# A fused attention and mixture-of-experts layer on one core: three edits to the order of work in its first pass

## The reference

```python
x = x + _layernorm(attn(_layernorm(x)))     # RWKV-like attention
x = x + _layernorm(moe(_layernorm(x)))      # 8 experts, the best 2 of each token, and one shared MLP

# attention: xk, xv, xr are mixtures of x and x shifted by one token
k, v, r = xk @ Wk.T, xv @ Wv.T, xr @ Wr.T
sr = sigmoid(r)
# scan over the tokens, a and b carried per channel
eku = exp(u + kt); out = (a + eku * vt) / (b + eku)
ek = exp(kt);      a, b = a * ew + ek * vt, b * ew + ek
attn = (sr * out) @ Wo.T

# moe: top 2 of softmax(x @ gate_w.T + gate_b); each expert and the shared MLP:
h = silu(x @ w1.T + b1) * (x @ w3.T + b3);  y = h @ w2.T + b2
```

## Time and profile before

| | us |
|---|---|
| median of 3 runs | 1219.38 |
| lowest, highest | 1210.02, 1220.20 |
| the profiled execution | 1216.82 |
| its span, first to last instruction | 1215.0 |
| TensorE busy (matmul) | 1007.6 (83%) |
| DVE busy | 847.6 (70%) |
| POOL busy | 795.2 (65%) |
| ACT busy | 569.0 (47%) |
| mean granted clock of TensorE | 0.922 |

### The profile page before, as it was taken

The page is one execution under the profiler, slowest core; times in us unless marked ns, Lnnn a source line. Parts: engine busy times, 40 slices in busy tenths (PEclk is TensorE's granted clock), DMA queues, the critical chain, the costliest instruction groups (busy, mean ns, idle before and its releaser), DMA issues. The chain is left out here.

```text
span 1215.0 us, 23017 instructions
## 1 busy us (share of the span) xinstructions
PE 1007.6 (83%) x6344; PEld 890.1 (73%) x6344; DVE 847.6 (70%) x2227; ACT 569.0 (47%) x1013; POOL 795.2 (65%) x790
## 2 busy tenths in 40 slices
PE   0567799999999999999997784979998999989562
PEld 0456678777877788778876674979998999988432
DVE  4577797778787888778876323746775766766496
ACT  4333664456555654565455423424443434433275
POOL 2233877787778777887787432447775766655498
PEclk9778999999999999999998877989998999999655
DMA  3223332453235423442243118588878888887496
GB/s 132 72 96 97 104 108 83 138 160 125 73 123 160 130 81 118 152 143 91 96 135 105 62 68 286 135 218 200 155 136 220 161 197 193 188 209 192 104 262 223
DMA packets 114548, 174.05 MB, mean 143 GB/s; under 512 B 13485, under 2 KB 93768, under 8 KB 112200
## 3 DMA queue, kind: packets, MB, share of 16 engines
q1 hardware_dynamic: 83304, 121.09, 32.9%
q0 software_dynamic: 26592, 35.67, 15.8%
q10 hardware_dynamic: 4608, 16.78, 3.7%
HBM read 173.53 MB, written 78.21 MB: 207 GB/s over the span
## 5 line engine op out<-in xcount | busy, mean ns | idle before, releaser
L1497 POOL DMA_INDIRECT sum_y<-e_y,e_row_at x142 | 222.5, 1567 | 44.2 <-issue 40.7
L1331 PE MATMUL e_h_ps<-e_z_hi,e_w 128*128 128x256 f32 x1136 | 222.6, 290 | 29.1 <-DMA e_w<-w_split 17.5
L1331 PEld LDWEIGHTS e_h_ps<-e_z_hi,e_w 128*128 128x128 f32 x1136 | 187.1, 197 | 31.9 <-issue 22.4
L1331 PE MATMUL e_h_ps<-e_z_lo,e_w 128*128 128x256 f32 x568 | 163.7, 288 | 0.0
L1373 ACT ACTIVATE e_act_h<-e_h_ps,e_w 128x256 f32<-128x256 f32 x142 | 67.3, 474 | 205.6 <-PE e_h_ps L1331 182.8
L1152 POOL DMA_INDIRECT slots_x<-f_xf,f_at x128 | 140.3, 1096 | 32.4 <-issue 32.4
L615 PE MATMUL f_h_ps<-f_f_hi,f_w_hi 128*128 128x512 f32 x256 | 108.9, 425 | 27.7 <-DVE f_h L909 23.8
L1412 DVE SCALAR_TENSOR_TENSOR e_h<-e_h_ps,e_w,e_act_h 128x256 f32<-128x256 f32 x142 | 68.1, 483 | 75.7 <-ACT e_act_h L1373 63.1
L1347 PE MATMUL e_y_ps<-e_w,e_h_hi 128*128 128x256 f32 x568 | 118.4, 292 | 1.1 <-DVE e_h_lo L1419 1.1
L876 DVE RECIPROCAL f_den<-f_den 128x256 f32<-128x256 f32 x64 | 111.6, 1746 | 1.1
L1331 PEld LDWEIGHTS e_h_ps<-e_z_lo,e_w 128*128 128x128 f32 x568 | 111.9, 197 | 0.0
(11 more groups left out here) (222 smaller groups left out, 2971.3 us busy)
## 6 DMA issues: line engine op xcount, KB each, us to landing
e_w<-w_split SPq DMA_DIRECT2D x71, 1026.0 KB
e_w<-w_split ACTq DMA_DIRECT2D x71, 512.0 KB
e_x_in<-slots_x SPq DMA_DIRECT2D x71, 260.0 KB
f_x_in<-x SPq DMA_DIRECT2D x16, 512.0 KB, 5.0
f_x_res<-x SPq DMA_DIRECT2D x16, 512.0 KB, 5.9
x_dram<-f_x SPq DMA_DIRECT2D x16, 512.0 KB, 6.6
sum_y<-f_y SPq DMA_DIRECT2D x32, 256.0 KB, 3.0
c_x<-x_dram SPq DMA_DIRECT2D x32, 256.0 KB
```

The lines of the kernel that those rows point to most:

```text
L1331: last = pe.matmul(h_ps[q][:, which, :], w13(p, part)[:, which, c, q * P:(q + 1) * P], z[p % 2][:, c, :], start=(n == 0), stop=(n == 5))
L1497: pool.indirect_dma_start(out=dst[:, :], out_offset=bass.IndirectOffsetOnAxis(ap=row_at[p][:, j:j + 1], axis=0), in_=y[p][:, j, :], in_off ...
```

## The change

Five places in `first_pass`:

- DVE: `product(i - 2, 2)` moves ahead of `denominator(i, 1)`; the second half's reciprocal becomes one instruction of 512 columns behind `low(i + 1)`, instead of one half in front of the product and one behind `low`. The count that `gate` waits for goes with it, from 4 to 3 per sequence.
- DVE and ACT: `low_w` and `high_w` move from the end of the step to its start, `low_w` behind `moments_x`, `high_w` behind the first `f_high`.
- SP: the stores of the split weights move ahead of the loads of `x_in` and `x_res`, the store of x1 and the `zs` transfers; the load of `w_raw` moves to the end of the body and is for the next step.
- Pool: `running_sums(i, 1)` and `inverse_std` of the third norm move ahead of the hold and the first two scatters.

```diff
@@ SP
             def body(i, par):
-                if inside(i, SEQS):
-                    wait(sp, w_stored, 64 * i)
-                    sp.dma_start(w_raw[:, :], expert_w[:, bass.ds(i * HALF_W, HALF_W)]).then_inc(w_loaded, 16)
...
+                if inside(i, SEQS):
+                    half = i % 2 if isinstance(i, int) else par
+                    sp.wait_ge(w_lo_ready, i + 1)
...
+                n = i + 1
+                if inside(n, SEQS):
+                    wait(sp, w_stored, 64 * n)
+                    sp.dma_start(w_raw[:, :], expert_w[:, bass.ds(n * HALF_W, HALF_W)]).then_inc(w_loaded, 16)
@@ ACT
                 f_high(i - 2, par, 0)
+                high_w(i)
                 exps(i, 0)
...
                 read_y(i - 3, 1)
-                high_w(i)
                 h_high(i - 2, 0)
@@ DVE
-                dve.wait_ge(rec_ready, 4 * s + n)
+                dve.wait_ge(rec_ready, 3 * s + n)
...
                 moments_x(i + 1, 1 - par)
+                low_w(i)
                 f_low(i - 2, par, 1)
...
                 aggregate(LN_X1, i - 1, 1 - par)
+                product(i - 2, 2)
                 denominator(i, 1)
-                invert(i, 1, slice(0, T // 2))
-                product(i - 2, 2)
-                low_w(i)
                 low(i + 1)
-                invert(i, 1, slice(T // 2, T))
-                gate(i, 1, 4)
+                invert(i, 1, slice(0, T))
+                gate(i, 1, 3)
@@ POOL
                 add_x(i - 1, 1 - par)
+                running_sums(i, 1)
+                inverse_std(LN_X1, i - 1, 1 - par)
                 if inside(i - 2, SEQS):
                     hold(pool, scratch, held, i - 2, (at_ready, i - 1))
                 send(i - 2, par, 0, (0, 1))
-                running_sums(i, 1)
-                inverse_std(LN_X1, i - 1, 1 - par)
```

More of the change, by code:

```diff
@@ L466, in body @@
                             .then_inc(y_stored[half], 16)
+                if inside(i, SEQS):
+                    half = i % 2 if isinstance(i, int) else par
+                    sp.wait_ge(w_lo_ready, i + 1)
+                    for low, words in ((0, w_high[:, :].bitcast(F32)), (1, w_raw[:, :])):
+                        if half == 0:
+                            at = i * (W_ALL // 2) + low * W13
+                            sp.dma_start(w_split[:, bass.ds(at, HALF_W)], words).then_inc(w_stored, 32)
+                        else:
+                            at = (i - 1) * (W_ALL // 2)
+                            sp.dma_start(w_split[:, bass.ds(at + low * W13 + HALF_W, W13 - HALF_W)],
+                                         words[:, 0:W13 - HALF_W]).then_inc(w_stored, 16)
+                            sp.dma_start(w_split[:, bass.ds(at + 2 * W13 + 4 + low * W2, W2)], words[:, W13 - HALF_W:])\
+                                .then_inc(w_stored, 16)
                 n = i + 2
```

## The result

| | before | after |
|---|---|---|
| median of all runs, us | 1216.58 | 1225.27 |
| lowest, highest | 1210.02, 1222.80 | 1222.71, 1233.62 |
| ratio, 95% interval | 1 | 1.0079 [1.0064, 1.0095] |
| span of the profiled execution | 1215.0 | 1225.3 |
| mean granted clock of TensorE | 0.922 | 0.909 |

The third of the projections starts at 140.83 after and at 147.10 before: filling the pipe gained 6.3 us, where 6.6 were forecast. The last one starts at 676.36 against 662.86: the middle has lost all that and 13.5 us more.

What follows compares the result with a forecast made beforehand. TensorE was taken to wait on DVE's order, then on Pool: a middle step falls from 39.70 to 38.65 us. Gains 2.5 + 3.1 + 1.0 + 12 x 1.05 = 19.2 us off 1216.8 give 1197.6, set at 1200; range 1186 to 1214.

Steps and rivals of the forecast that it cites:

- The two waits of TensorE: TensorE's waits in ten steps, 14.9 us for DVE's `f_h` and 7.2 us for `f_z_lo`; both were to go.
- that for `f_den`: DVE's denominator sat idle 2.26 us for Pool's `f_den`; that wait was to be gone.
- Filling the pipe: First steps of the first pass: gains of 2.5, 3.1 and 1.0 us in steps 0, 1 and 2.
- Pool idles 2.3 us for the scan: Pool, after its `f_x` addition, was to wait 2.3 us for `f_a_sum`, which follows DVE's scan.
- Pool's chain from the running sums to the end of `g_low`: Pool's work before the projection: 18.4 us was to shrink to 16.35 through fewer meetings with DVE.
- P+22.3: Middle step, counted from the projection's start P: when `f_a_sum` ends and Pool's running sums can start.
- P+38.7: Middle step, counted from the projection's start P: when Pool's chain lets the next projection start.
- the term for SP in the sum: SP's weight stores (issues of 1.1 to 1.8 us) fit its idle time ahead of `zs_hi`; counted as 0.
- Rival (b): First pass: thinner cover, late weights or `g_low` waiting for DVE; 8 us of gain left, 1211; chance 0.27.
- 1.5 us of waiting to spend: TensorE's expected wait for Pool in front of the projection, about 1.5 us, which delays could use up without cost.
- the clock was forecast to stand: TensorE's clock, at 1.00 with a wait of 1.54 us each step, should stay with a like wait elsewhere.
- The rival's late weights: Part of the 0.27 rival: weights landing late delay ACT's exponentials, the second `f_low` and the logits.

Runs made afterwards that it cites:

- e1: The changed kernel with the stores of the split weights first in SP's body, ahead of the stores of y; 1201.8 us, ratio 0.9887.
- e2: The changed kernel with the whole weight split (loads, stores, `high_w`, `low_w`) as before, `low_w` right ahead of `low`; 1203.5 us, ratio 0.9892.
- e12: The changed kernel with the `zs` transfers on ACT's queue and SP waiting for `f_z_lo` before the next weight load; 1233.2 us, ratio 1.0123.
- e8: The kernel before with Pool's part alone: running sums and scales ahead of the hold and first two scatters; 1213.2 us, ratio 0.9992.
- e7: The kernel before with DVE's part alone: product q=2 ahead of the denominator, whole reciprocal behind `f_z_lo`; 1196.3 us, ratio 0.9843.
- e3: The changed kernel with Pool's order as before: hold and two scatters ahead of the running sums; 1222.2 us, ratio 1.0027.
- e5: The changed kernel with the weight stores first on SP and Pool's order as before; 1189.2 us, ratio 0.9787.
- e6: The changed kernel with the stores of the split weights issued from ACT's queue instead of SP's; 1209.6 us, ratio 0.9965.

## Why the prediction was wrong

**What held.** The two waits of TensorE and that for `f_den` are gone. Filling the pipe gained 1.6, 3.3 and 1.4 us at the first three projections where 2.5, 3.1 and 1.0 were forecast. Pool idles 2.3 us for the scan. Pool's chain from the running sums to the end of `g_low`, forecast at 16.35 instead of 18.4, takes 16.1 in the changed kernel, 16.2 in e1 and 16.7 in e2, where a scatter is still held up (1.52 for 0.96). In e2, without the weight split's move, the running sums start at P+22.1 and the projection is due at P+38.8; forecast were P+22.3 and P+38.7. That part of the sum was right to 0.3 us a step: e2's step is 38.95 against 38.65, its time 1203.5 against 1200.

**What failed** is the term for SP in the sum, "I take nothing": the stores of the weights in front of `zs` were put at 0 and cost TensorE a wait of 2.5 us a step. The reasoning asked whether SP's queue had time for the issues, and it had: the idle time in front of `zs_hi` took them in. It did not ask whether the engines behind the queue had room for the bytes. The windows of before show that they had not: shares of 0.97 to 1.09 up to 338.4, as shown above. 0.79 MB at the 239 to 390 GB/s of those windows are 2.0 to 3.3 us, and by the prediction's own sum `f_z_lo` was to come 2.5 us earlier as well (336.0 and not 338.6). The price, per step, from the rows: the wait of 2.5, the low clock behind it 1.4 (from the wait's end to the projection's start 4.1 us, 2.7 for the same matmuls in e1), less the waits that e1 has in its place, 0.3 for `zs`, 0.9 for `f_g_lo` and 0.7 for `f_mask`: 2.0, and the measured distance from e1 is 41.44 - 39.34 = 2.1. Over the first pass and its end that is the 26 us between the two spans, 1225.3 and 1199.1.

**The rival that had it.** Rival (b) named the transfers behind the stores, but priced them at 8 us of remaining gain, because "TensorE has 1.5 us of waiting to spend". That slack was 0.9 us, it is spent on a wait of 2.5, and the clock was forecast to stand, by a wait of 1.54 that had left it at 1.00; it fell and cost 1.4 us a step more. The rival's late weights came true as well (ACT waits 24.6 us for them in ten steps, 2.1 in e1), but not as what TensorE waits for. The rule of the Trainium skill that stood beside it, page "DMA: Bandwidth & Descriptors", section "Queues, rings and completion order" (descriptors are taken in ring order), pointed to the right transfers; but e12 shows that here another queue would not have saved them. The rival's other half, the weight subtraction against Pool, came true with the roles exchanged: not `g_low` waited for DVE but, in e1, DVE for `g_low` and `h_low`, 1.7 us instead of the 0.95 feared. The step of e1 is 0.4 above that of e2 (39.34, 38.95); how much of that is the subtraction's is not shown, as e1 also differs in SP's order, and TensorE's wait for `f_mask`, 0.7 a step in e1, is there with the subtraction in its old place too (4.7 us in ten steps in e8, 5.2 in e7).

**Not seen.** The prediction's own numbers had Pool's reordering as no gain (22.35 + 16.35 = 38.70 against 20.07 + 18.4 = 38.47 unchanged) and didn't say so. Measured, it costs 1.05 a step in the changed kernel (41.44 against 40.39 in e3) and 1.0 with SP's order mended. The change as a whole was forecast, its parts were not; e7 and e5 are the better kernels. The prediction also counted from the median of three runs, 1219.4, where 18 give 1216.6; from that its sum would give about 1197, so this does not explain the miss.

## What to carry to other kernels

A DMA has two places in line, its queue and the engines: before bytes are moved ahead of a small transfer that somebody waits for, read the DMA share of the windows up to its issue, and count what other engines' transfers will move in them; near 1, what stands in front costs its time at the measured rate, and here another queue did not get round it. A prefetch or a write-back belongs where the share is low, here at the start of a step. And forecast each part of a change by itself: two reorderings that mend the same wait do not add up (e7 and e8 against e2), and one can cost what the other gains.

## What the runs showed of the hardware

- With all engines full (share 1.0 to 1.1, up to 399 GB/s in a window of 2 us of e12), the last of the small transfers, issued by 339.36 on a queue of its own, was waited for until 345.23. Its queue had 34% of the engines from 340 to 344, and none before, 3.9 us after its first issue.
- Under that load the issue of a small transfer takes longer too: for the first of the two of `f_zs_lo` on SP 461/462/526 ns (shortest/median/longest) before, 461/1036/1980 after.
- TensorE's granted clock stood at 1.00 with a wait of 1.54 us in each step before, and fell to 0.50 for some 3 us behind each of the waits of 2.0 to 4.0 after, though in both kernels the engine is busy for over 93% of the middle. The length of the wait alone does not decide it: it also fell behind one of 1.90 in e6, and not behind one of 2.03 in e6, of 2.31 in e3 and of 2.67 in e12. A matmul of 128x512 in the middle of such a stretch takes 0.63 us and not 0.39.
- A two-input operation of DVE of 0.95 us took 2.65 to 2.86 when two of Pool's operations stood back to back across it, and 4.15 with three (e1).
